# Norm, FP4 rounding and layer 1's key norm taken by pairs of tiles instead of groups of four, in a two-layer transformer kernel on one core

## The reference, cut to what matters

```python
h = _layernorm(x, axis=-1) * (1 + ca) + sa
x = x + ga * _L0_attn_ref(h, Wq, Wk, Wv)      # rotary, causal (one beyond the diagonal), softmax
h = _layernorm(x, axis=-1) * (1 + cb) + sb    # norm 1
x = x + gb * _L0_ffn_ref(h, ...)              # three linear maps, inputs and weights rounded to FP4
h = _layernorm(x, axis=-1) * (1 + ca) + sa    # norm 2: layer 1's queries, keys and values
x = x + ga * _L1_attn_ref(h, qk, ov)
h = _layernorm(x, axis=-1) * (1 + cb) + sb    # norm 3
x = x + gb * _L1_ffn_ref(h, ...)              # router, 8 experts, one shared

def fp4_quant_dequant(x):                     # blocks of 16 along the last dimension
    scale = jnp.maximum(jnp.max(jnp.abs(xb), axis=-1, keepdims=True) / 6.0, 1e-12)
    return _GRID[jnp.searchsorted(_MID, jnp.abs(xb / scale))] * jnp.sign(xb) * scale
```

## Time and profile before

| | before |
|---|---|
| median of 3 runs | 708.12 us (707.89 to 708.6) |
| the profiled execution, from its first to its last instruction | 705.9 us |
| mean granted TensorE clock in it | 0.986 of full speed (2.4 GHz) |
| instructions in it | 11080 |
| busy: PE, DVE, ACT, POOL | 633.8, 476.2, 340.6, 239.6 us |

### The profile page before, as it was taken

One profiled execution on the slowest core, in us unless ns is written; L12 is line 12 of the kernel. 1 busy time (PEld: TensorE's weight loads), 2 busy tenths in 40 slices (PEclk: granted clock), 3 DMA queues, 4 the chain that ended last, 5 costly groups with the idle time before them and its releaser, 6 DMA issues.

```text
span 705.9 us, 11080 instructions
## 1 busy us (share of the span) xinstructions
PE 633.8 (90%) x3839; PEld 487.1 (69%) x3839; DVE 476.2 (67%) x1270; ACT 340.6 (48%) x701; POOL 239.6 (34%) x320
## 2 busy tenths in 40 slices
PE   5799899988779899998899999869889998998996
PEld 4366687877556778775678777746768875676774
DVE  5965589786687557626569886688555527766665
ACT  1133464565535464433455465444555544454553
POOL 3424756462754211004557464484310002000000
PEclk9989999999999999999999999999999999999999
DMA  8200000000000000000000000100000000001011
GB/s 272 61 1 1 2 1 1 1 1 1 1 0 1 3 0 1 1 2 1 1 0 1 2 0 1 37 22 1 0 1 1 1 1 1 1 15 31 15 31 30
DMA packets 12174, 9.65 MB, mean 14 GB/s; under 512 B 1804, under 2 KB 10840, under 8 KB 12120
## 3 DMA queue, kind: packets, MB, share of 16 engines
q1 hardware_dynamic: 12120, 8.95, 4.2%
HBM read 6.84 MB, written 2.10 MB: 13 GB/s over the span
## 4 chain that ended last, share of the span: by engine, by line
PE 62%; DVE 21%; ACT 8%; issue 5%; POOL 3%; DMA 1%; SPq 0%; ACTq 0%; POOLq 0%; DVEq 0%
PE ps L840 13%; PE ps L705 10%; PE ps L818 8%; PE ps L990 4%; PE ps L992 4%; PE ps L991 4%; PE ps L664 4%; PE ps L863 2%; PE ps L864 2%; PE ps L725 2%; ACT xn L1108 2%; PE ps L659 2%; PE ps L879 2%; DVE row_max L1441 2%; POOL rstd L518 2%
## 5 line engine op out<-in xcount | busy, mean ns | idle before, releaser
L1172 ACT ACTIVATE probsT<-ps 128x512 f32<-128x512 f32 (+3 forms) x160 | 85.2, 533 | 158.4 <-PE ps L818 158.4
L840 PE MATMUL ps<-v_sb,probsT 128*128 128x129 f32 (+1 forms) x1124 | 151.4, 279 | 3.7 <-ACT probsT L1174 3.7
L840 PEld LDWEIGHTS ps<-v_sb,probsT 128*128 128x128 f32 (+1 forms) x1124 | 137.6, 191 | 8.8 <-ACT probsT L1174 5.5
L1441 DVE TENSOR_REDUCE row_max<-ps 128x1 f32<-128x512 f32 (+2 forms) x144 | 87.4, 619 | 51.2 <-PE ps L713 26.5
L818 PE MATMUL ps<-ident,probs 128*128 128x128 f32 (+1 forms) x562 | 90.2, 276 | 15.7 <-ACT hT L1100 7.8
L1146 ACT ACTIVATE probs<-ps,neg_max 128x512 f32<-128x512 f32 (+7 forms) x158 | 93.0, 620 | 10.4 <-DVE neg_max L1448 8.2
L818 PEld LDWEIGHTS ps<-ident,probs 128*128 128x128 f32 (+1 forms) x562 | 63.1, 139 | 47.6 <-issue 44.0
L554 POOL TENSOR_TENSOR hq<-ha,hp 128x352 f32<-128x352 f32 x32 | 29.8, 932 | 108.2 <-DVE hp L1491 108.2
L705 PE MATMUL ps<-k_high,q_high 128*128 128x512 f32 (+5 forms) x100 | 42.5, 425 | 6.0 <-ACT probs L1146 6.0
L659 PE MATMUL ps<-unpick,ident_b 128*128 128x512 bf16 x196 | 47.4, 383 | 0.3 <-ACT v_sb L1238 0.3
L517 POOL TENSOR_SCALAR minus_mean<-mv 128x4 f32<-128x4 f32 (+1 forms) x16 | 3.8, 237 | 121.5 <-DVE veps L1309 121.3
(11 more groups left out here) (245 smaller groups left out, 1390.0 us busy)
## 6 DMA issues: line engine op xcount, KB each, us to landing
out<-x_sb SPq DMA_DIRECT2D x8, 256.0 KB, 2.3
x_sb<-in_L_attn_x SPq DMA_DIRECT2D x2, 512.0 KB, 5.2
hT_all<-in_L_wmod SPq DMA_DIRECT2D x2, 384.0 KB
rope_cos<-table_cos SPq DMA_DIRECT2D x1, 768.0 KB, 6.3
rope_sin<-table_sin SPq DMA_DIRECT2D x1, 768.0 KB, 7.8
rope_cos<-table_cos SPq DMA_DIRECT2D x1, 256.0 KB, 3.4
rope_sin<-table_sin SPq DMA_DIRECT2D x1, 256.0 KB, 5.0
moe_raw<-in_L_ffn_expert_gate_w SPq DMA_DIRECT2D x1, 256.0 KB, 2.7
```

The source lines that it names most:

```text
L840: mm = pe.matmul(bank(OUT_AT, 0, V_W), probsT[0:size, n % 4, k * P:(k + 1) * P], v_sb[0:size, j, :], start=(c == 0 and k == 0), stop=(c == ...
L1172: ins = act.activation(probsT[:, n % 4, 0:full], bank(TURN, 0, full), ACT.Copy)
L1441: ins = dve.tensor_reduce(dst, ps[:, start:start + width], AX.X, ALU.max, negate=single)
```

## The change

Two tiles, not four, are the unit from the statistics to the transposes in norm 1, and from the statistics to `normalise_2` in norm 2. Pair p holds tiles 2p and 2p+1.

- `send_statistics` and `scale_and_shift` run in every odd slot, over two tiles and the one or two kinds of norm.
- `normalise_1` of pair p is done at the end of slot 2p+2 on ACT, `normalise_2` of pair p at the end of slot 2p+10, both after everything else of the slot.
- `modulate_1` of pair p is done on POOL in slot 2p+3.
- `fp4_input` of pair p is done on DVE in slot 2p+3, ahead of `quantise_h` and `finish`, over 256 columns.
- `xq_scaled` of pair p is done on POOL in slot 2p+4, ahead of `hq_scaled`.
- "fp4_first" holds tiles 0 and 1 of a group and stays in slot 4g+6; "fp4_rest" holds tiles 2 and 3 and goes from slot 4g+7 to 4g+8.
- The transposes of norm 2 stay by groups of four, where they were. So do norm 0 and norm 3; norm 3 waits for the counts of the pairs.

```diff
-FP4_PARTS = ((0, 1), (1, GROUP))
+PAIR = 2
+PAIRS_OF_TILES = TILES // PAIR
+FP4_PARTS = ((0, PAIR), (PAIR, GROUP))
+def pair_at(slot, first):
+    p, off = divmod(slot - first, PAIR)
+    return p if off == 0 and 0 <= p < PAIRS_OF_TILES else None
-    firsts = (("fp4_first", FFN_LAG), ("fp4_rest", FFN_LAG + 1), ...
+    firsts = (("fp4_first", FFN_LAG), ("fp4_rest", FFN_LAG + PAIR), ...
+NORM1_PAIR_SLOT, NORM2_PAIR_SLOT = PAIR, DOWN_LAG + PAIR
+FP4_PAIR_SLOT = PAIR + 1
+XQ_PAIR_SLOT = PAIR + 2
-NORM_GROUPS = (2 * GROUPS, 2 * GROUPS, GROUPS)
+RSTD_PAIRS = SLOTS // PAIR
 # POOL
-            def scale_and_shift(kinds, n):
-                rows = slice(0, kinds)
+            def scale_and_shift(kinds, pair, n):
+                rows, cols = slice(0, kinds), slice(pair * PAIR, (pair + 1) * PAIR)
...
-                def modulate_1(g):
+                def modulate_1(p):
...
-                    for t in range(GROUP):
+                    for t in range(PAIR):
...
-                def xq_scaled(g):
-                    pool.wait_ge(xq_grid, b * GROUPS + g + 1)
+                def xq_scaled(p):
+                    g, part = divmod(p, 2)
+                    done = b * PAIRS_OF_TILES + p
+                    pool.wait_ge(xq_grid, done + 1)
                     if g >= 1:
-                        pool.wait_ge(turned, TURN_AT[b, "fp4_rest", g - 1] + 1)
-                    for part, (a, z) in enumerate(FP4_PARTS):
+                        pool.wait_ge(turned, TURN_AT[b, ("fp4_first", "fp4_rest")[part], g - 1] + 1)
+                    a, z = FP4_PARTS[part]
...
-                    if at(NORM1_SLOT + 1) is not None:
-                        modulate_1(at(NORM1_SLOT + 1))
+                    if pair_at(s, NORM1_PAIR_SLOT + 1) is not None:
+                        modulate_1(pair_at(s, NORM1_PAIR_SLOT + 1))
+                    if pair_at(s, XQ_PAIR_SLOT) is not None:
+                        xq_scaled(pair_at(s, XQ_PAIR_SLOT))
                     if ffn_tile(s, FFN_LAG) is not None:
                         hq_scaled(s - FFN_LAG)
...
-                    if s % GROUP == GROUP - 1:
-                        scale_and_shift(1 + (at(NORM2_SLOT) is not None), b * 2 * GROUPS + s // GROUP + 1)
+                    if s % PAIR == PAIR - 1:
+                        scale_and_shift(1 + (ffn_tile(s, DOWN_LAG) is not None), s % GROUP // PAIR, b * RSTD_PAIRS + s // PAIR + 1)
...
-                    if at(FP4_SLOT) is not None:
-                        xq_scaled(at(FP4_SLOT))
 # PE, gate_up
-                    if t < 2:
-                        out_of_bank((("fp4_first", "fp4_rest")[t], g))
+                    if t % PAIR == 0:
+                        out_of_bank((("fp4_first", "fp4_rest")[t // PAIR], g))
 # ACT
-                def normalise_1(g):
-                    act.wait_ge(shift_ready, b * 2 * GROUPS + g + 1)
-                    for t in range(GROUP):
-                        normalise(0, t, g).then_inc(xn1_ready, 1)
+                def normalise_1(p):
+                    act.wait_ge(shift_ready, b * RSTD_PAIRS + p + 1)
+                    for t in range(p * PAIR, (p + 1) * PAIR):
+                        normalise(0, t % GROUP, t // GROUP).then_inc(xn1_ready, 1)
+                def normalise_2(p):
+                    g, part = divmod(p, 2)
+                    if g > 1 and part:
                         act.wait_ge(xn_ready, b * len(XN_AT) + XN_AT["norm2", g])
+                    act.wait_ge(shift_ready, b * RSTD_PAIRS + DOWN_LAG // PAIR + p + 1)
...
-                        if c == min(1, turns - 1) and group_at(s, NORM1_SLOT + 1) is not None:
-                            normalise_1(group_at(s, NORM1_SLOT + 1))
                     if s >= FP4_SLOT:
                         round_ropes(s)
-                    if group_at(s, NORM2_SLOT + 1) is not None:
-                        normalise_2(group_at(s, NORM2_SLOT + 1))
+                    if pair_at(s, NORM1_PAIR_SLOT) is not None:
+                        normalise_1(pair_at(s, NORM1_PAIR_SLOT))
+                    if pair_at(s, NORM2_PAIR_SLOT) is not None:
+                        normalise_2(pair_at(s, NORM2_PAIR_SLOT))
 # DVE
-                    if s % GROUP == GROUP - 1:
+                    if s % PAIR == PAIR - 1:
                         link(ins)
-                        send_statistics(0, 1 + (ffn_tile(s, DOWN_LAG) is not None), link)
+                        first = s % GROUP // PAIR * PAIR
+                        send_statistics(0, 1 + (ffn_tile(s, DOWN_LAG) is not None), link, (first, first + PAIR))
...
-                def fp4_input(g):
+                def fp4_input(p):
+                    g, part = divmod(p, 2)
+                    a, z = (t * P for t in FP4_PARTS[part])
+                    done = b * PAIRS_OF_TILES + p
                     def scales_used():
-                        if g:
-                            dve.wait_ge(xq_ready, 2 * (b * GROUPS + g))
+                        if done >= 2:
+                            dve.wait_ge(xq_ready, done - 1)
-                    dve.wait_ge(h_shifted, b * TILES + (g + 1) * GROUP)
-                    quantise(qa[:], qp[:], xn[:, g, :], GROUP * P // BLOCK, qs, scales_used).then_inc(xq_grid, 1)
+                    dve.wait_ge(h_shifted, b * TILES + (p + 1) * PAIR)
+                    quantise(qa[:, a:z], qp[:, a:z], xn[:, g, a:z], (z - a) // BLOCK,
+                             qs[:, :, a // BLOCK:z // BLOCK], scales_used).then_inc(xq_grid, 1)
...
+                    if pair_at(s, FP4_PAIR_SLOT) is not None:
+                        fp4_input(pair_at(s, FP4_PAIR_SLOT))
                     if ffn_tile(s, FFN_LAG) is not None:
                         quantise_h(s - FFN_LAG)
...
                     finish(s)
-                    if group_at(s, FP4_SLOT) is not None:
-                        fp4_input(group_at(s, FP4_SLOT))
```

More of the change, by code:

```diff
@@ L112, in input_turns @@
 def input_turns(batch, slot):
-    firsts = (("fp4_first", FFN_LAG), ("fp4_rest", FFN_LAG + 1), ("norm2", DOWN_LAG + GROUP + 1), ("norm3", TILES + GROUP + 2))
+    firsts = (("fp4_first", FFN_LAG), ("fp4_rest", FFN_LAG + PAIR), ("norm2", DOWN_LAG + GROUP + 1), ("norm3", TILES + GROUP + 2))
     turns = [(kind, group_at(slot, first)) for kind, first in firsts if group_at(slot, first) is not None]
@@ L516, in scale_and_shift @@
                     pool.wait_ge(shift_ready, n - 1)
-                pool.tensor_scalar(minus_mean[:, rows, :], mv[:, rows, :, 0], -1.0, None, ALU.mult)
-                pool.tensor_tensor(rstd[:, rows, :], veps[:, rows, :], half[:, rows, :], ALU.pow).then_inc(rstd_ready[0], 1)
+                pool.tensor_scalar(minus_mean[:, rows, cols], mv[:, rows, cols, 0], -1.0, None, ALU.mult)
+                pool.tensor_tensor(rstd[:, rows, cols], veps[:, rows, cols], half[:, rows, cols], ALU.pow).then_inc(rstd_ready[0], 1)
                 pool.wait_ge(rstd_ready[0], n)
-                pool.tensor_tensor(shift[:, rows, :], minus_mean[:, rows, :], rstd[:, rows, :],
+                pool.tensor_tensor(shift[:, rows, cols], minus_mean[:, rows, cols], rstd[:, rows, cols],
                                    ALU.mult).then_inc(shift_ready, 1)
@@ L533, in _ @@
             for b in range(BATCH):
-                def modulate_1(g):
-                    tiles = [xn[:, g, t * P:(t + 1) * P] for t in range(GROUP)]
-                    first = b * TILES + g * GROUP
+                def modulate_1(p):
+                    tiles = [xn[:, t // GROUP, t % GROUP * P:(t % GROUP + 1) * P] for t in range(p * PAIR, (p + 1) * PAIR)]
+                    first = b * TILES + p * PAIR
                     def add_shift(t):
@@ L547, in modulate_1 @@
                             add_shift(t - 1)
[L548 removed]
+                    add_shift(PAIR - 1)
                 def hq_scaled(n):
@@ L1300, in at_least_quarter, with send_statistics @@
                 link(dve.tensor_tensor(dst, up, low, ALU.add))
-            def send_statistics(kind, kinds, link):
+            def send_statistics(kind, kinds, link, tiles=(0, GROUP)):
                 for n in range(kind, kind + kinds):
-                    for k in range(GROUP):
+                    for k in range(*tiles):
                         ins = dve.bn_aggr(mv[:, n, k, :], bn[:, n, k, :])
                 link(ins)
-                rows = slice(kind, kind + kinds)
-                dve.tensor_scalar(veps[:, rows, :], mv[:, rows, :, 1], LN_EPS, None, ALU.add).then_inc(var_ready[kind // 2], 1)
+                rows, cols = slice(kind, kind + kinds), slice(*tiles)
+                dve.tensor_scalar(veps[:, rows, cols], mv[:, rows, cols, 1], LN_EPS, None, ALU.add).then_inc(var_ready[kind // 2], 1)
             def first_tile(batch, t):
```

28 lines of the change are left out of this document (13 added, 15 removed).

## The result

| | before | after |
|---|---|---|
| median | 708.34 us (4 executions) | 718.26 us (4 executions, 714.76 to 720.42) |
| ratio | | 1.0138, 95% interval 1.0106 to 1.0171 |
| profiled execution, its span | 705.9 us | 717.2 us (its time: 720.42) |
| mean granted clock in it | 0.986 | 0.978 |
| instructions | 11080 | 11220 |

The change made the kernel 9.9 us slower, against 8.4 forecast. The two numbers are near each other, but that is in part luck: more than half of the loss is a lower TensorE clock, of which the forecast says nothing, and the waits that it did price cost less than it said.

What follows compares the result with a forecast made beforehand. TensorE was 90% busy with 62% of the chain, DVE setting the end in stretches. Per batch 2.5 - 0.4 + 0.9 + 0 + 1.1 + 0.8 - 0.7 = 4.2 us, twice 8.4; 705.9 + 8.4 + 2.2 gives 716.5 us, range 708 to 720.5.

Steps and rivals of the forecast that it cites:

- 18 to 20: Slot 17's q_low on DVE: the group's burst gone, the pair and sending added; -0.4 us a batch, bounds -1.3 and +0.3.
- 21 to 31: Norm 2's transposes on PE: the three waits for xn go; -0.7 us a batch.
- Slot 13, the pair and the sending: DVE ahead of q_low: pair +2.05, sending statistics +0.5, together +2.5 us on PE's wait, bounds 2.0 and 3.4.
- Slot 7: DVE waits for POOL's modulate_1, delaying shift, norm, exponential and PE in slot 8; +0.9 us a batch, bounds 0 and +2.
- Slots 10 and 14, ACT ahead of the exponential: Four normalise (1.64 us) at slot end delay PE's scores; +1.1 and +0.8 us a batch, bounds of each 0 and 1.6.
- PE's 2.9 us there stay: Slot 17's step: PE's wait for q_low, 2.9 us before the change, was to remain.
- Slots 1 to 6: Modulation in slots 3 and 5 falls into DVE's idle time, slot 5's exponential wait shrinks by 0.5; 0, bounds -1 and +1.
- the bound that it names: Slot 13's high bound, 3.4 us, taken in both batches with the rest as forecast, given for the upper end 720.5.
- 1.8 in slot 8 less 0.8 in slot 9: Slot 7's step: PE 1.8 us late in slot 8, slot 9 giving back PE's 0.8 us wait; summed as +0.9.
- Only the DVE term is real: Rival: exponentials don't gate PE so directly, slot 7 settles in DVE's idle time; +2.8, 710.9 us (708.7 to 713), chance 0.27.
- Faster: the bursts were the bound: Rival: without DVE's bursts behind finish PE's waits go; 702.7 us (700 to 706.7), decided ending slots 8 and 10, chance 0.14.
- The rule weighed in the prediction: On DVE, SBUF latency is paid per instruction, so tiles should be at least 512 elements; splitting costs 1.1 us a group.

Runs made afterwards that it cites:

- e4_filler: The changed kernel, with 14 and 12 matmuls that nobody reads ahead of PE's waits for q_low in slots 14 and 18; 708.57 us, ratio 0.9993.
- e1_fp4_late: The changed kernel with all pairs' fp4_input (DVE) and xq_scaled (POOL) one slot later; 735.17 us, ratio 1.0385.
- c4_slot7: c3_send with pair 2's fp4_input on DVE in slot 7 moved from ahead of quantise_h to behind finish; 694.18 us, ratio 0.9774.
- c3_send: The changed kernel with fp4_input of pairs 5, 7 and sending of slots 13, 17 behind q_low, fillers, normalise_1 and half of normalise_2 mid-slot; 697.96 us, 0.9863.
- e2_act_mid: The changed kernel with ACT's normalise_1 of all pairs and normalise_2 of each group's first pair moved to mid-slot; 715.24 us, ratio 1.0095.

## Why the prediction was right, and where it was not

To set its steps against what happened I take the time from DVE's division by the row sum (once a slot) in one slot to that in another, less the same in the same batch of the kernel before. One execution each. e4_filler stands for the change with its clock kept up, but only partly: in the first batch the clock still fell behind slot 9's scores, and in the second the kernel before had its own fall in slots 18 to 20. So the last column takes e4_filler's second batch, and its first batch for slots 18 to 20.

| slots | predicted | after, first batch | e4_filler, first | e4_filler, second | without a fall |
|---|---|---|---|---|---|
| 1 to 6 | 0 | -1.65 | -1.64 | -1.63 | -1.63 |
| 7 to 9 | +0.9 | +2.15 | +2.13 | +1.26 | +1.26 |
| 10 to 12 | +1.1 | +1.48 | +1.49 | +0.68 | +0.68 |
| 13, 14 | +2.5 | +3.85 | +2.51 | +2.51 | +2.51 |
| 15 to 17 | +0.8 | -0.60 | -0.60 | -0.59 | -0.59 |
| 18 to 20 | -0.4 | +1.88 | +0.72 | -0.67 | +0.72 |
| 21 to 31 | -0.7 | -1.00 | -1.10 | -1.14 | -1.14 |
| sum | +4.2 | +6.11 | +3.51 | +0.42 | +1.81 |

- **The sum was right by luck.** The steps that the forecast did price cost about 1.8 us a batch with the clock up, against 4.2 forecast. In the slots of both batches the changed kernel lost 13.5 us (6.1 and 7.4), so the clock was by far the larger part in that execution. It was also the slowest of the four.
- **Slot 13, the pair and the sending.** The pair was put at 2.05 us and took 1.93, and e1_fp4_late gave just that back. The sending was put at 0.5 and took 1.07: the forecast took veps at its median of 0.17 us, and it took 0.74, beside POOL's rounding of hq (at 100.78 in slot 7 it took 0.94, for as long as the instruction of POOL beside it). The maximum of 814 ns stood in the earlier trace rows and should have been asked where it came from; there, too, POOL was rounding hq. PE's wait is 4.52 for "about 4": it grew by 3.0, just the pair and the sending. With the clock kept the two slots are only 2.51 longer, the 2.5 that was summed; what gave 0.5 back isn't traced.
- **Slot 7.** DVE's wait for POOL (1.59 for 1.5), POOL's shift behind hq(1), ACT's norm and exponential behind it: all came as described, PE's wait being 1.42 for 1.8. The price was right too: slots 7 to 12 cost 1.9 without a fall of the clock, forecast 2.0. The 3.6 of the first batch hold 1.7 of clock. c4_slot7 takes this one chain away and gains 0.9% of the time over c3_send, the clock behind it included.
- **Slots 10 and 14, ACT ahead of the exponential.** Both waits are 1.12 us, for 1.1 and 0.8. Slots 15 to 17 come out 0.6 us shorter than before all the same. PE's waits for the copy of xqT (0.31) and for xq (0.77) are gone, which makes up for the new one; what gave the 0.6 beyond that stays open. The forecast let q_low in slot 18 eat the wait for xq, and so it was: PE's wait there grew from 2.91 to 3.71 us, though "PE's 2.9 us there stay". Slots 15 to 20 together cost +0.1 with the clock kept, forecast +0.4. The wait in slot 14 costs its full length: e2_act_mid, without it, has slots 15 to 17 another 1.4 us shorter.
- **Slots 1 to 6** were put at 0, bounds -1 and +1, and gave 1.6 back. PE's wait before slot 6's scores fell from 1.61 to 0.80, more than the 0.5 forecast. The low clock behind it went too (0.66 before, 1.00 after, over 75 to 80 us), but it had cost next to nothing: in the kernel before these slots took 45.57 us in the first batch with it and 45.44 in the second without it.
- **The clock.** This is what the sum lacked. The forecast priced a wait by its own length. e4_filler gives 9.7 us back by filling the waits; the kernel before gives 4.9; so the change added about 5 us of clock. With filler in both kernels the change costs 0.9993 / 0.9936, 0.6% or 4 us, of which some is clock still, by the fall that e4_filler kept. By the slots it is 2 x 1.8, less some 1.1 gained between the batches and behind them: 2.5. The forecast had 8.4 for that. So the real 9.9 is 2.5 to 4 us of stalls and 6 to 7 of clock. Too high a sum of direct terms (the gains in slots 1 to 6 and 15 to 17 were left out) covered for a term that wasn't there.
- **The bounds.** The range's upper end, 720.5, doesn't follow from the bound that it names: 716.5 + 2 x 0.9 is 718.3. And 1.8 in slot 8 less 0.8 in slot 9 is 1.0, not 0.9.
- **The rivals.** "Only the DVE term is real" falls with e2_act_mid, where ACT's old place gives 3.0 us back, the clock behind its waits included. "Faster: the bursts were the bound" was wrong of this change. It was to decide at the end of slots 8 and 10; c4_slot7, where the first of these waits is down to 0.62 us and the second, for probs, has become one of 0.68 for a copy, is 1.6% faster than the groups with filler, but its other edits have a part in that.
- **Splitting on DVE.** The rule weighed in the prediction (the Trainium skill, "VectorE: DVE Perf Modes", "The TRN2 errata") holds in kind: the scaling took 425 ns at 256 columns, beside 524 at 352 and 691 at 512, so some 160 of them don't depend on the columns, near the page's text and not its table. But two pairs, 3.86 us of instructions, took only 0.5 more than a group had, 3.37, since the groups were slowed beside POOL; 1.1 was forecast. DVE's busy time is up 8.4 us for "some 9", again by luck; its main parts are 3.9 from the pairs' six instructions, 7.3 from veps (40 instead of 24, many of them slow beside POOL), 5.5 less for `quantise_h`. The split isn't what made the kernel slower: c4_slot7 pays the same.

## What to carry to other kernels

Price a stall on TensorE by its length and by what the clock does behind it: here the second was larger than the first, and the granted clock of a stretch and the mean of one group of matmuls show it. Before a finer unit of work is judged, move each new piece behind whatever TensorE waits for in that slot, on every engine in order; the same pairs cost 1.4% in one order and gained 2.3% in another, part of that gain being filler and moves that would be open to groups too. A wait that can't be removed can be filled with matmuls that nobody reads, if they end before it does.

## What the runs showed of the hardware

- The granted clock fell behind waits of PE as short as 1.42 us (0.66 in the stretch behind it), 1.61 us (0.66) and 1.79 us (0.69, then 0.63), but not behind each: the kernel before has the same wait of 2.91 us in both batches, and 1.00 behind the first, 0.66 behind the second; e4_filler has 1.42 and 1.41 us, with 0.66 and 1.00 behind them. What decides between them stays open.
- One such fall cost 1.7 us in e4_filler (slots 7 to 12), 1.4 in the kernel before (slots 18 to 20) and 0.1 in its slots 1 to 6.
- 2.08 us more of waiting at one place, twice a run, cost 5.3 us with PE kept busy and 10.1 us without.
- DVE's veps (128x2 or 128x4) took 0.17 us by itself and up to 0.95 us while POOL rounded hq (128x352); the slow ones ended with POOL's instruction, within 0.03 us.
